# A routed-expert tail in fewer steps: logits made by tokens, fixed expert tiles indexed and gathered ahead of the spare ones, one batch's gated low parts on VectorE, routing masks by comparison

## The chip, the cores and the metric

The kernel runs on one core of a Trainium2 chip. The time is device microseconds of one execution. The core has five engines, which run their own instruction streams and wait for each other through semaphores: TensorE (PE in the profile; PEld is its weight load), VectorE (DVE), ScalarE (ACT), GpSimd (POOL) and SyncE (SP), which issues most of the DMA transfers.

## What is computed

Two batches of 512 tokens, 512 features wide, pass three residual blocks. All data are fp32.

```python
x = x + cross_attention(layernorm(x), ctx_1024)      # 8192 context rows, per batch
x = x + ssm(layernorm(x), ...)                        # long convolution by FFT, gated, clipped
x = x + ffn(layernorm(x), gate_w, gate_b, expert_w, expert_b)

def ffn(x, gate_w, gate_b, expert_w, expert_b):       # 8 experts of 512 x 512
    logits = xt @ gate_w + gate_b
    gates = softmax(logits)
    sel = argmax(gates)                               # one expert for each token
    onehot = one_hot(sel, 8)
    y_all = einsum('td,edh->eth', xt, expert_w) + expert_b[:, None, :]
    out = einsum('te,eth->th', onehot, y_all)
```

## The kernel before

The program is one long stream for each engine, written out by hand; there is no scheduler. It falls into a preparation of weights, an attention over the context for each batch, and a tail. The change is in the tail, the last 150 us.

Every result in PSUM is a job. The list `JOBS` sets the order of the jobs on TensorE and with it the bank of each (the number of the job modulo 8); a job waits until the job that had its bank before has been read. Large products are made of operands that are split into a high and a low part (`hl_A` to `hl_F`, fp32r): ScalarE rounds the high part, and VectorE or GpSimd subtracts to get the low part. A product is then 12 matmuls of 512 columns.

The tail, from about 978 us of the span on, does this:

- `outputs(c, groups)` on VectorE multiplies the spectra of the second batch (helper line 376 of the profile), `outputs_lo` (line 1810) takes low parts, `gate_output` (line 1823) gates the time signal. The low parts of the gated signal, `gated_lo`, are made on GpSimd for the first batch (line 2167) and on VectorE for the second (line 1815).
- `project_out` on TensorE (line 644) makes `x_ssm`, and `add_output` on VectorE adds it to the residual, tile by tile of 128 tokens, eight tiles.
- For each tile `turn_ffn` (line 978) transposes the sum on TensorE and ScalarE copies it (line 1224) into `spectra`. Both wait behind `weights(3)` in ScalarE's stream, which rounds expert matrix 3 once its DMA has landed.
- `gate_logits` (line 987) multiplies with the gate's weights. `gate_raw`, 8 columns, is the stationary operand, the tokens are the moving one, 512 or 256 at a time, so that the logits come out with experts on partitions. ScalarE copies them (line 1228), and `turn_logits` (line 998) transposes them to tokens on partitions.
- `scale_outputs`, `split_expert_bias` (lines 1895 to 1898) and `gate` (from line 1873) on VectorE give the one-hot of the chosen expert. `rank_tokens` on TensorE (lines 1007 to 1010) counts with two 0/1 masks, `before` and `ones`, where in its expert's queue each token stands. GpSimd makes the masks in `routing_masks` (lines 2192 to 2197).
- `route` on VectorE turns ranks into a place. There are 15 tiles of 128 places: 8 fixed ones, one for each expert, and 7 spare ones for what is over. It writes a 128x1024 0/1 matrix `place` (line 1928), `place_tokens` on TensorE (line 1017) makes the list of rows from it, and `gather_rows` and `scatter_rows` are converted (lines 1932, 1934).
- GpSimd gathers the rows of a tile with an indirect DMA (line 2202), after everything has been stored to `mixed` (`norm_stored`, `x_stored`). For each tile TensorE transposes the tokens (`turn_tokens`, line 1026), ScalarE rounds them (line 1347), VectorE takes the low part (line 1957), and `mix` multiplies with the expert's matrix (line 1040) and adds the bias (line 1045). GpSimd scatters the result (line 2209).

SyncE issues the loads and stores of this part in one fixed order: expert matrices 0, the bias, 1, 2 and 4, the store of x of batch 0, matrices 3 and 5, the store of x of batch 1, four stores of normalized rows, matrices 6 and 7, and then those of the spare tiles. GpSimd's order after the masks is: add the output bias to the residual of batch 1 (line 2162), low parts of matrices 0 to 3 (line 2023), gathers.

## Time and profile before

| | us |
|---|---|
| median of 3 executions | 1134.09 (1133.72 to 1135.25) |
| the profiled execution | 1134.54 |
| its span | 1132.8 |
| TensorE busy | 1093.9 (97%) |
| VectorE busy | 841.3 (74%) |
| ScalarE busy | 530.5 (47%) |
| GpSimd busy | 537.5 (47%) |

The span goes from the first to the last instruction of the trace, the execution's own time has 1.7 us around it. A busy share is a mean over a long program: in the stretch from 1040 to 1060 us TensorE is busy 12.4 of 20 us, and from 1060 to 1080 12.5 of 20. All times in this text are us from the span's start unless something else is said.

### The profile page before, as it was taken

What the parts mean: (1) busy time and instruction counts of PE and PEld (TensorE: products, weight loads), DVE (VectorE), ACT (ScalarE), POOL (GpSimd) and SP (SyncE); (2) the same over time, 40 slices, a digit from 0 to 9 for tenths busy, and PEclk for the clock granted to TensorE, in tenths of its full rate; (3) what the DMA queues carried; (4) which work ended last, traced back from release to release, by engine and by line L of the source; (5) the groups of instructions that cost most, each with busy time, mean ns of one, the idle gap of its engine ahead of it and who ended that gap; (6) DMA issues with size and microseconds to landing.
All of it is one profiled execution on the core that took longest, in us unless ns stands there. A gap on an engine that the chain in (4) does not pass through costs nothing.

```text
span 1132.8 us, 16497 instructions
## 1 busy us (share of the span) xinstructions
PE 1093.9 (97%) x4969; PEld 884.5 (78%) x4969; DVE 841.3 (74%) x1756; ACT 530.5 (47%) x1127; POOL 537.5 (47%) x588
## 2 busy tenths in 40 slices
PE   7999999999999999999999999999999999998498
PEld 5787877878888888888888888888888888886375
DVE  6963498799888888778357777776777657699584
ACT  4221056556555555533464444444444444356462
POOL 3700445345444544411266666665765632177253
PEclk8999999999999999999999999999999999999699
DMA  8211368977876787432429767766876541025991
GB/s 292 84 53 59 52 153 211 218 194 190 204 179 185 190 192 195 140 87 99 76 73 203 193 187 202 187 191 171 213 185 177 179 161 38 1 76 161 323 398 66
DMA packets 199351, 182.26 MB, mean 161 GB/s; under 512 B 17873, under 2 KB 144881, under 8 KB 199299
## 3 DMA queue, kind: packets, MB, share of 16 engines
q1 hardware_dynamic: 178658, 140.21, 48.3%
q10 hardware_dynamic: 17280, 31.46, 7.9%
q0 software_dynamic: 3360, 9.97, 2.4%
q8 instruction: 24, 0.39, 0.1%
q14 instruction: 29, 0.23, 0.1%
HBM read 141.73 MB, written 41.68 MB: 162 GB/s over the span
## 4 chain that ended last, share of the span: by engine, by line
PE 80%; DVE 8%; POOL 4%; DMA 3%; issue 3%; SPq 1%; ACT 1%; POOLq 0%; ACTq 0%; DVEq 0%
PE bank L644 39%; PE bank L783 28%; PE bank L1040 4%; PE bank L837 3%; PE bank L652 1%; PE bank L1026 1%; DMA stage<-in_L_xattn_hW_dram 1%; DVE h L1527 1%; DMA stage<-in_L_ffn_expert_w_dram 1%; DMA spectra<-in_ctx_dram 1%; PE bank L987 1%; PE bank L678 1%; POOL hl_C L2023 1%; PE bank L1045 1%; POOL hl_B L2039 1%
## 5 line engine op out<-in xcount | busy, mean ns | idle before, releaser
L1187 ACT ACTIVATE probs<-bank,nbias 128x512 f32<-128x512 f32 x128 | 88.1, 688 | 242.3 <-DVE nbias L1650 242.1
L783 PE MATMUL bank<-hl_F,probsT 128*128 128x512 f32 x768 | 190.4, 397 | 0.6 <-issue 0.4
L783 PE MATMUL bank<-hl_A,probsT 128*128 128x512 f32 x768 | 190.4, 396 | 0.0
L644 PE MATMUL bank<-hl_B,hl_D 128*128 128x512 f32 x768 | 185.7, 391 | 1.8 <-POOL hl_B L2039 1.4
L1645 DVE TENSOR_REDUCE mx<-bank 128x1 f32<-128x512 f32 x128 | 88.0, 687 | 133.9 <-PE bank L644 133.9
L644 PE MATMUL bank<-hl_C,hl_D 128*128 128x512 f32 x768 | 185.3, 390 | 0.0
L783 PEld LDWEIGHTS bank<-hl_F,probsT 128*128 128x128 f32 x768 | 144.1, 188 | 35.4 <-issue 0.8
L783 PEld LDWEIGHTS bank<-hl_A,probsT 128*128 128x128 f32 x768 | 144.1, 188 | 34.3 <-POOL hl_A L2032 0.2
L644 PEld LDWEIGHTS bank<-hl_B,hl_D 128*128 128x128 f32 x768 | 143.7, 188 | 34.1 <-issue 2.3
L644 PEld LDWEIGHTS bank<-hl_C,hl_D 128*128 128x128 f32 x768 | 144.1, 188 | 31.7 <-issue 0.3
L2032 POOL TENSOR_TENSOR hl_F<-stage,hl_F 128x512 fp32r<-128x512 f32 x64 | 84.7, 1323 | 162.2 <-ACT hl_F L1152 162.1
L2032 POOL TENSOR_TENSOR hl_A<-stage,hl_A 128x512 fp32r<-128x512 f32 x64 | 84.2, 1315 | 145.4 <-ACT hl_A L1152 145.4
L1691 DVE SCALAR_TENSOR_TENSOR rows<-rows,alpha,bank 128x512 f32<-128x512 f32 x128 | 90.9, 710 | 14.9 <-PE bank L783 14.9
L1662 DVE TENSOR_TENSOR probsT<-bank,probsT 128x512 fp32r<-128x512 f32 x128 | 87.3, 682 | 1.9 <-ACT probsT L1174 1.8
L1174 ACT ACTIVATE probsT<-bank 128x512 fp32r<-128x512 f32 x128 | 74.2, 580 | 10.8 <-PE bank L770 10.7
L1152 ACT ACTIVATE hl_F<-stage 128x512 fp32r<-128x512 f32 x64 | 40.4, 632 | 27.7 <-issue 18.2
L1152 ACT ACTIVATE hl_A<-stage 128x512 fp32r<-128x512 f32 x64 | 40.4, 632 | 27.6 <-issue 18.3
L2039 POOL TENSOR_TENSOR hl_C<-spectra,hl_C 128x512 fp32r<-128x512 f32 x32 | 40.9, 1292 | 22.9 <-ACT hl_C L1160 22.9
L2039 POOL TENSOR_TENSOR hl_C<-xb,hl_C 128x512 fp32r<-128x512 f32 x32 | 41.0, 1292 | 20.2 <-ACT hl_C L1160 20.2
L1667 DVE STREAM_TRANSPOSE bank<-resid 128x512 f32<-128x512 f32 x60 | 43.0, 716 | 9.4 <-DMA resid<-p_rows 9.4
L1683 DVE SCALAR_TENSOR_TENSOR lsum<-lsum,alpha,rsum 128x1 f32<-128x1 f32 x128 | 49.0, 383 | 0.0
L1699 DVE SCALAR_TENSOR_TENSOR zT<-h,cbdt,zT 128x512 f32<-128x512 f32 x64 | 46.6, 728 | 0.0
(419 smaller groups left out, 1862.6 us busy)
## 6 DMA issues: line engine op xcount, KB each, us to landing
p_rows<-probs ACTq DMA_DIRECT2D x120, 256.0 KB, 3.1
stage<-in_ctx_dram SPq DMA_DIRECT2D x112, 256.0 KB, 3.2
spectra<-in_ctx_dram SPq DMA_DIRECT2D x64, 256.0 KB, 5.9
xb<-in_ctx_dram SPq DMA_DIRECT2D x64, 256.0 KB, 5.9
resid<-p_rows SPq DMA_DIRECT2D x240, 64.0 KB, 2.1
h<-p_rows SPq DMA_DIRECT2D x120, 64.0 KB, 2.5
obB<-p_rows SPq DMA_DIRECT2D x120, 64.0 KB, 2.0
stage<-in_L_ffn_expert_w_dram SPq DMA_DIRECT2D x6, 1024.0 KB, 6.9
```

The source lines that it names most:

```text
L644: last = nc.tensor.matmul(dst, lhs[:, a, t, k * P:(k + 1) * P], rhs[:, c, t, :], start=(t == 0 and (a, c) == PASSES[0]), stop=(t == T - 1 ...
L783: last = nc.tensor.matmul(obank[u % 2][:], probsT[u % 2][:, a, j, :], nat[b][par][:, c, j, :], start=(j == 0 and (a, c) == PASSES[0]), sto ...
L1152: nc.scalar.activation(nat[b][par][:, 0, j, :], stage[par][:, j, :], ACT.Copy).then_inc(nat_hi, 1)
L1174: nc.scalar.activation(dst, src, ACT.Copy).then_inc(pT_hi, 1)
L1187: nc.scalar.activation(dst, src, ACT.Exp, bias=nbias[:, q:q + 1], scale=SCALE, accum_out=rsum[:, q:q + 1]).then_inc(probs_ready, 1)
L1645: nc.vector.tensor_reduce(mx[:, col], sbank[u % 2][:], AX_X, ALU.max).then_inc(stat_done, 1)
L1662: nc.vector.tensor_tensor(lo, src, hi, ALU.subtract).then_inc(pT_split, 1)
L1683: nc.vector.scalar_tensor_tensor(lsum[:, col], lsum[:, col], alpha[:, u:u + 1], rsum[:, col], ALU.mult, ALU.add).then_inc(sums_updated, 1)
L1691: nc.vector.scalar_tensor_tensor(rows[:, q, :], rows[:, q, :], alpha[:, u:u + 1], obank[u % 2][:], ALU.mult, ALU.add).then_inc(rows_added, 1)
L1699: nc.vector.scalar_tensor_tensor(kern[:, k, :], h[u % 2][:], weight, kern[:, k, :], ALU.mult, ALU.add).then_inc(term_added, 1)
L2032: nc.gpsimd.tensor_tensor(nat[b][par][:, 1, j, :], stage[par][:, j, :], nat[b][par][:, 0, j, :].bitcast(F32), ALU.subtract).then_inc(nat_s ...
L2039: nc.gpsimd.tensor_tensor(by_squares(ctxT[par][:, 1])[:, dd], square(squares[b][par], dd), by_squares(ctxT[par][:, 0])[:, dd].bitcast(F32) ...
```

## The change

The change has seven parts.

1. `gate_logits` swaps its operands: for each tile of 128 tokens the tokens are now the stationary operand (128 columns, four times, one for each 128 features), and `gate_raw` with its 8 columns is the moving one. The logits come out with tokens on partitions. The copies and `turn_logits` are gone. The logits of a tile follow two tiles behind its transposes.
2. `route` writes `place` twice: first by rank alone, for the fixed tiles, which `slots.0` turns into the rows of tiles 0 to 7, and then by lane, for the spare tiles (`slots.1`). GpSimd may gather tiles 0 to 7 after the first.
3. `split_expert_bias` moves from ahead of `gate` to behind `route`.
4. `turn_tokens(1)` moves from ahead of `mix(0)` into it, behind its first 3 matmuls.
5. The low parts of the first batch's gated signal move from GpSimd to VectorE, between groups 2 and 3 of the products.
6. `routing_masks` makes each mask with one comparison or multiply-add from `lanes`, without the wait for VectorE's products.
7. GpSimd takes the low part of expert matrix 0 ahead of the bias of batch 1, after a wait for VectorE's products.

The diff, cut to its core:

```diff
-             + tiles_at(0, "x_ssm")[2:] + tiles_at(1, "x_ssm") + tiles_at(0, "ffnT") + tiles_at(1, "ffnT")[:2]
-             + ["logits@0"] + tiles_at(1, "ffnT")[2:] + ["logits@1", "logit_columns", "ranks", "slots"] + MIX_JOBS)
+             + tiles_at(0, "x_ssm")[2:] + tiles_at(1, "x_ssm") + tiles_at(0, "ffnT") + tiles_at(1, "ffnT")
+             + ["logit_columns", "ranks"] + (["slots.0", "slots.1"]) + MIX_JOBS)
...
-                for t in range(T):
-                    turn_ffn(0, t)
-                for t in range(2):
-                    turn_ffn(1, t)
-                gate_logits(0, 1)
-                for t in range(2, T):
-                    turn_ffn(1, t)
-                gate_logits(1, 2)
-                turn_logits()
+                for n in range(B * T + 2):
+                    if n < B * T:
+                        turn_ffn(n // T, n % T)
+                    if n >= 2:
+                        gate_logits(n - 2)
                 rank_tokens()
-                place_tokens()
+                place_tokens("slots.0", 1, 0, E)
+                place_tokens("slots.1", 2, E, E)
                 turn_tokens(0)
                 for g in range(GROUPS):
-                    if g + 1 < GROUPS:
+                    if 0 < g < GROUPS - 1:
                         turn_tokens(g + 1)
...
+            def gate_logits(n):
+
+                dst = bank_of("logit_columns")
+                if n == 0:
+                    open_bank("logit_columns")
+                evacuated_from(f"ffnT.{n % T}@{n // T}")
+                for k in range(T):
+                    last = nc.tensor.matmul(dst[:, n * E:(n + 1) * E], spectra[:, n, k * P:(k + 1) * P], gate_raw[:, k, :],
+                                            start=(k == 0), stop=(k == T - 1))
+                if n == B * T - 1:
+                    last.then_inc(filled, 1)
...
+
+                pe.wait_ge(ranked, count)
+                dst = open_bank(job)
                 for n in range(B * T):
-                    last = nc.tensor.matmul(dst[:, 0:2 * E], place[:, n, :], numbered[:, n, :], start=(n == 0), stop=(n == B * T - 1))
+                    last = nc.tensor.matmul(dst[:, 0:width], place[:, n, :], numbered[:, n, first:first + width],
+                                            start=(n == 0), stop=(n == B * T - 1))
...
@@ -1039,6 +1028,8 @@
                     for a, c in PASSES:
                         nc.tensor.matmul(dst[:], tokens_hl[g % 2][:, a, t, :], weights[:, c, t, :],
                                          start=(t == 0 and (a, c) == PASSES[0]), stop=False)
+                    if g == 0 and t == 0:
+                        turn_tokens(1)
...
                 turned_ffn(0, range(T))
-                turned_ffn(1, range(2))
-                copy_logits(0)
-                turned_ffn(1, range(2, T))
-                copy_logits(1)
+                turned_ffn(1, range(T))
...
+            def gated_lo(b, k):
+                dve.wait_ge(gated_hi_done[b], k + 1)
+                nc.vector.tensor_tensor(gated_hl[b][:, 1, k, :], z[b][:, k, :], gated_hl[b][:, 0, k, :].bitcast(F32),
+                                        ALU.subtract).then_inc(gated_lo_done[b], 1)
...
+                nc.vector.tensor_tensor(numbered[:, :, 0:E], hits.bitcast(F32), of_token(token), ALU.mult)
                 link(nc.vector.tensor_tensor(hit_value, hits.bitcast(F32), of_expert(numbers[:, 0:E]), ALU.mult))
                 link(nc.vector.tensor_reduce(own, hit_value, AX_X, ALU.add))
...
-                nc.vector.tensor_reduce(rank, hit_value, AX_X, ALU.add)
+                link(nc.vector.tensor_reduce(rank, hit_value, AX_X, ALU.add))
+                place_at(rank)
                 link(nc.vector.tensor_tensor(above, count.unsqueeze(2).to_broadcast([P, E, SPARE]),
                                              limits.unsqueeze(1).to_broadcast([P, E, SPARE]), ALU.is_gt))
                 link(nc.vector.tensor_reduce(tiles_over, above, AX_X, ALU.add))
-                nc.vector.tensor_tensor(above, rank.unsqueeze(2).to_broadcast([P, B * T, SPARE]),
-                                        limits.unsqueeze(1).to_broadcast([P, B * T, SPARE]), ALU.is_ge)
                 link(nc.vector.tensor_tensor_scan(tiles_upto, unit, tiles_over, 0.0, ALU.mult, ALU.add))
+                filled_by(dve, "slots.0")
+                nc.vector.tensor_scalar(gather_rows[:, 0:E], bank_of("slots.0")[:, 0:E], float(FAR), float(TOKENS - 1),
+                                        ALU.add, ALU.min).then_inc(indexed, 1)
+                nc.vector.tensor_scalar(scatter_rows[:, 0:E], bank_of("slots.0")[:, 0:E], float(FAR), None, ALU.add).then_inc(evacuated, 1)
+                link(nc.vector.tensor_tensor(above, rank.unsqueeze(2).to_broadcast([P, B * T, SPARE]),
+                                             limits.unsqueeze(1).to_broadcast([P, B * T, SPARE]), ALU.is_ge))
                 nc.vector.tensor_reduce(over, above, AX_X, ALU.add)
                 link(nc.vector.scalar_tensor_tensor(extra, tiles_upto, float(E - 1), tiles_over, ALU.add, ALU.subtract))
-                nc.vector.scalar_tensor_tensor(lane, over, -float(P), rank, ALU.mult, ALU.add)
-                link(nc.vector.tensor_tensor(hit_value, hits.bitcast(F32), extra.unsqueeze(1).to_broadcast([P, B * T, E]), ALU.mult))
-                nc.vector.tensor_tensor(count, over, own, ALU.subtract)
+                link(nc.vector.scalar_tensor_tensor(lane, over, -float(P), rank, ALU.mult, ALU.add))
+                nc.vector.tensor_tensor(hit_value, hits.bitcast(F32), extra.unsqueeze(1).to_broadcast([P, B * T, E]), ALU.mult)
+                link(nc.vector.tensor_tensor(count, over, own, ALU.subtract))
                 link(nc.vector.tensor_reduce(rank, hit_value, AX_X, ALU.add))
                 link(nc.vector.tensor_tensor(count, count, rank, ALU.add))
                 link(nc.vector.scalar_tensor_tensor(count, over, 0.0, count, ALU.is_gt, ALU.mult))
                 link(nc.vector.tensor_tensor(group, count, own, ALU.add))
-                link(nc.vector.tensor_tensor(hit_group, group.unsqueeze(2).to_broadcast([P, B * T, 2 * E]),
-                                             numbers.unsqueeze(1).to_broadcast([P, B * T, 2 * E]), ALU.is_equal))
-                nc.vector.tensor_tensor(numbered, hit_group, token.unsqueeze(2).to_broadcast([P, B * T, 2 * E]), ALU.mult)
-                nc.vector.tensor_tensor(place, lane.unsqueeze(2).to_broadcast([P, B * T, P]),
+                link(nc.vector.tensor_tensor(hit_group, group.unsqueeze(2).to_broadcast([P, B * T, E]),
+                                             numbers[:, E:2 * E].unsqueeze(1).to_broadcast([P, B * T, E]), ALU.is_equal))
+                nc.vector.tensor_tensor(numbered[:, :, E:2 * E], hit_group, token.unsqueeze(2).to_broadcast([P, B * T, E]), ALU.mult)
+                place_at(lane)
+                choose_experts()
+                filled_by(dve, "slots.1")
+                nc.vector.tensor_scalar(gather_rows[:, E:GROUPS], bank_of("slots.1")[:, 0:SPARE], float(FAR), float(TOKENS - 1),
+                                        ALU.add, ALU.min).then_inc(indexed, 1)
+                nc.vector.tensor_scalar(scatter_rows[:, E:GROUPS], bank_of("slots.1")[:, 0:SPARE], float(FAR), None, ALU.add).then_inc(evacuated, 1)
+
+            def place_at(m):
+
+                nc.vector.tensor_tensor(place, m.unsqueeze(2).to_broadcast([P, B * T, P]),
                                         lanes.unsqueeze(1).to_broadcast([P, B * T, P]), ALU.is_equal).then_inc(ranked, 1)
...
@@ -1977,7 +1971,10 @@
                 outputs(1, range(1))
                 outputs_lo(0)
                 gate_output(0, range(2, T))
-                outputs(1, range(1, 5))
+                outputs(1, range(1, 3))
+                for k in range(T):
+                    gated_lo(0, k)
+                outputs(1, range(3, 5))
                 outputs_lo(1)
...
                 output_means(1)
                 dve.wait_ge(means_ready, 1)
                 scale_outputs()
-                split_expert_bias()
                 gate()
                 route()
+                split_expert_bias()
                 for g in range(2):
                     turned_lo(g)
                     weight_los(g + EARLY)
...
@@ -2187,14 +2178,9 @@
             def routing_masks():

                 filled_by(pool, "U1i.1@1")
-                pool.wait_ge(product_step, PRODUCTS * (TRIPS + 2))
-                whole = obB[:, 2 * P:3 * P]
-                chain(nc.gpsimd.memset(whole, 1.0))
-                nc.gpsimd.tensor_copy(ones, whole).then_inc(table_made, 1)
-                pool.wait_ge(table_made, 1)
-                chain(nc.gpsimd.affine_select(out=whole, in_=whole, compare_op=ALU.is_gt, fill=0.0, base=0,
-                                              pattern=[[1, P]], channel_multiplier=-1))
-                nc.gpsimd.tensor_copy(before, whole).then_inc(table_made, 1)
+                pool.wait_ge(iota_made, 1)
+                nc.gpsimd.tensor_scalar(ones, lanes, 0.0, 1.0, ALU.mult, ALU.add).then_inc(table_made, 1)
+                nc.gpsimd.tensor_scalar(before, lanes, partition, None, ALU.is_gt).then_inc(table_made, 1)
...
                 outputs_lo()
                 routing_numbers()
                 add_out_bias(0)
-                gated_lo()
                 routing_masks()
+                pool.wait_ge(product_step, PRODUCTS * (TRIPS + 2))
+                lo_tiles("W0", raw[BUF["W0"]], weights_hl[0])
                 add_out_bias(1)
-                for g in range(EARLY):
+                for g in range(1, EARLY):
                     lo_tiles(f"W{g}", raw[BUF[f"W{g}"]], weights_hl[g])
                 pool.wait_ge(x_stored, 16 * B)
                 pool.wait_ge(norm_stored, 16 * B * 2)
@@ -2225,6 +2212,7 @@
                 pool.wait_ge(indexed, 1)
                 for g in range(ROWS_KEPT):
                     gather(g)
+                pool.wait_ge(indexed, 2)
```

TensorE, the tail behind `project_out` (`L978` and `L974` are `turn_ffn`, `L987` and `L984` are `gate_logits`, `xb` holds the sums, `spectra` their transposes). Before:

```order
L978 MATMUL bank<-ident,xb 128x128 [waits evacuated]
L978 MATMUL bank<-ident,xb 128x128 x3
L987 MATMUL bank<-spectra,gate_raw 8x512 [waits copied,evacuated]
L987 MATMUL bank<-spectra,gate_raw 8x512 x3
L978 MATMUL bank<-ident,xb 128x128 [waits evacuated]
L978 MATMUL bank<-ident,xb 128x128 x3
L978 MATMUL bank<-ident,xb 128x128 [waits evacuated,copied]
L978 MATMUL bank<-ident,xb 128x128 x3
L987 MATMUL bank<-spectra,gate_raw 8x256 [waits copied]
L987 MATMUL bank<-spectra,gate_raw 8x256 x3
L987 MATMUL bank<-spectra,gate_raw 8x256 [waits copied]
L987 MATMUL bank<-spectra,gate_raw 8x256 x3
```

And with the change, from the third tile on:

```order
L974 MATMUL bank<-ident,xb 128x128 [waits evacuated]
L974 MATMUL bank<-ident,xb 128x128 x3
L984 MATMUL bank<-gate_raw,spectra 128x8 [waits copied]
L984 MATMUL bank<-gate_raw,spectra 128x8 x3
L974 MATMUL bank<-ident,xb 128x128 [waits evacuated]
L974 MATMUL bank<-ident,xb 128x128 x3
```

Six tiles were transposed ahead of the first logits; now three are, and each further tile stands behind the logits of an earlier one. The multiplication of 8 by 512 columns has become 128 by 8. The two groups of transposes of logits (`L998`) no longer follow.

VectorE, the end of `route` (`dft` is `place` and `numbered`, `ssm_in` and `ssm_w` hold small tables, `probsT` is the low part of the first tile's tokens). Before:

```order
L1925 TENSOR_TENSOR h<-ssm_in,ssm_w 128x128 [waits link_done]
L1927 TENSOR_TENSOR dft<-h,ssm_w 128x128 [waits link_done]
L1928 TENSOR_TENSOR dft<-ssm_in,ssm_w 128x1024
L1939 TENSOR_TENSOR ssm_in<-ssm_in,ssm_w 128x56
L1941 TENSOR_REDUCE ssm_w<-ssm_in 128x7 [waits link_done]
L1942 TENSOR_SCALAR ssm_w<-ssm_w 128x7 [waits link_done]
L1943 CAST chosen_expert<-ssm_w 128x7 [waits link_done]
L1944 TENSOR_SCALAR selected<-ssm_w 16x15
L1932 TENSOR_SCALAR gather_rows<-bank 128x15 [waits filled]
L1934 TENSOR_SCALAR scatter_rows<-bank 128x15
L1957 TENSOR_TENSOR probsT<-bank,probsT 128x512 [waits rounded]
```

With the change, the first placing (`L1927`) and its rows (`L1901`):

```order
L1891 TENSOR_TENSOR ssm_in<-onehot,bank 128x64 [waits filled,link_done]
L1892 TENSOR_REDUCE ssm_in<-bank 128x8
L1894 TENSOR_REDUCE ssm_in<-ssm_in 128x8 [waits evacuated]
L1927 TENSOR_TENSOR dft<-ssm_in,ssm_w 128x1024 [waits link_done]
L1896 TENSOR_TENSOR ssm_in<-ssm_in,ssm_w 128x56
L1898 TENSOR_REDUCE ssm_in<-ssm_in 128x8 [waits link_done]
L1899 SCALAR_TENSOR_TENSOR ssm_in<-ssm_w,ssm_in 128x8 [waits link_done]
L1901 TENSOR_SCALAR gather_rows<-bank 128x8 [waits filled,link_done]
L1903 TENSOR_SCALAR scatter_rows<-bank 128x8
```

And the second placing, with what stands ahead of the first tile's low part:

```order
L1938 TENSOR_SCALAR selected<-ssm_w 16x15
L1921 TENSOR_SCALAR gather_rows<-bank 128x7 [waits filled]
L1923 TENSOR_SCALAR scatter_rows<-bank 128x7
L1880 CAST dft<-probs 16x512 [waits iota_made,in_eb]
L1881 TENSOR_TENSOR h<-probs,dft 16x512 [waits link_done]
L1882 SCALAR_TENSOR_TENSOR probs<-h,ssm_w 16x512 [waits link_done]
L1883 SCALAR_TENSOR_TENSOR dft<-dft,ssm_w,probs 16x512 [waits link_done]
L1951 TENSOR_TENSOR probsT<-bank,probsT 128x512 [waits rounded]
```

The matrix `place` is written right behind the ranks and again 18 instructions later; the four instructions of the bias (`L1880` to `L1883`) now stand between the rows of the spare tiles and the first tile's low part.

## Rows read from the trace of the kernel before

**Rows 1.** The chain in order of time, from 985: start, us, what.

```profile
1028.13 7.80 DMA stage<-in_L_ffn_expert_w_dram
...
1038.15 1.95 ACT spectra L1224 x4
...
1040.23 3.59 PE bank L987 x8
...
1049.59 0.24 DVE logit L1876
...
1053.71 0.22 DVE ssm_in L1906
...
1057.27 1.15 DVE dft L1928
...
1058.46 1.89 PE bank L1017 x8
...
1060.37 0.18 DVE gather_rows L1932
...
1063.02 5.79 DMA spectra<-mixed,gather_rows
```

**Rows 2.** Timeline of VectorE: start, us, line, operation, count [idle before, releaser].

```profile
1001.54 1.67 DVE L376 TENSOR_TENSOR spectra<-probs,obB 128x512 f32<-128x512 f32 x1
...
1006.52 0.68 DVE L376 TENSOR_TENSOR obB<-resid,spectra 128x512 f32<-128x512 f32 x1
1007.12 0.68 DVE L376 TENSOR_TENSOR probs<-resid,spectra 128x512 f32<-128x512 f32 x1
...
1020.68 2.88 DVE L1815 TENSOR_TENSOR hl_A<-stage,hl_A 128x512 fp32r<-128x512 f32 x2
...
1043.76 0.41 DVE L1895 CAST dft<-probs 16x512 fp32r<-16x512 f32 x1
...
1046.36 0.20 DVE L1873 TENSOR_TENSOR ssm_in<-mv_out,gate_sums 128x64 f32<-128x64 f32 x1
```

**Rows 3.** Timeline of GpSimd.

```profile
994.20 11.85 POOL L2167 TENSOR_TENSOR hl_F<-zT,hl_F 128x512 fp32r<-128x512 f32 x4 [27.39 <-ACT hl_F L1288]
...
1010.00 2.16 POOL L2193 CAST dft<-obB 128x128 fp32r<-128x128 f32 x1
...
1017.85 6.85 POOL L2023 TENSOR_TENSOR hl_C<-stage,hl_C 128x512 fp32r<-128x512 f32 x4
```

**Rows 4.** Timeline of TensorE.

```profile
938.83 1.06 PE L897 MATMUL bank<-gate_raw,one 128*128 128x8 f32 x8
...
1034.63 2.78 PE L978 MATMUL bank<-ident,xb 128*128 128x128 f32 x24
...
1066.20 1.09 PE L1026 MATMUL bank<-ident,spectra 128*128 128x128 f32 x4 [5.86 <-DMA spectra<-mixed,gather_rows]
1068.95 1.09 PE L1026 MATMUL bank<-ident,spectra 128*128 128x128 f32 x4 [1.67 <-DMA spectra<-mixed,gather_rows]
...
1074.32 0.66 PE L1026 MATMUL bank<-ident,spectra 128*128 128x128 f32 x4
...
1078.14 0.66 PE L1026 MATMUL bank<-ident,spectra 128*128 128x128 f32 x4
```

**Rows 5.** Windows, TensorE alone: stretch, length, busy, granted clock, DMA share, GB/s.

```profile
931.90:938.80 6.90, 6.84 (x49) 1.00 0.32 123
...
1048.40:1051.90 3.50, 0.97 (x10) 1.00 0.51 195
...
1060.40:1066.10 5.70, 0.00 (x0) 0.50 0.94 326
```

**Rows 6.** Timeline of SyncE's DMA issues.

```profile
1053.27 1.77 SPq L560 DMA_DIRECT2D mixed<-zT  x2
```

**Rows 7.** Timeline of ScalarE.

```profile
1048.93 2.91 ACT L1330 ACTIVATE rows<-xb,ffn_shift,rstd 128x512 f32<-128x512 f32 x4
```

48 lines of the change are left out of this document (5 added, 43 removed).

## The prediction

> **What bounds the kernel now.** I read the page's busy lines first: TensorE is busy 97% of the whole span, so only a stretch where it waits can be shortened without taking work from it. The slices of the span show one, from 1036 to 1072. I followed the chain that ended last there in order of time, and then each engine's timeline. The reader is to see a relay [rows 1]: VectorE's work lets the load of expert matrix 3 start at 1028.13, it takes 7.80 us, ScalarE rounds that matrix and only then copies the transposed tiles (from 1038.15), TensorE multiplies them with the gate (from 1040.23), VectorE reads the logits at 1049.59, ranks at 1053.71, `place` at 1057.27, TensorE 1.89 us for the slots, rows at 1060.37, and a gather that took 5.79 us. From the second tile on TensorE repeats one pattern, 3.82 us a tile (1074.32 to 1078.14 [rows 4]), and waits for nothing: what arrives earlier at the first tile is worth its full amount at the end. The chain names GpSimd ahead of the load at 1028; the code says that the load stands behind the store of x of batch 0, which waits for VectorE's `add_output`. VectorE's own timeline has no idle time to speak of until it waits for the logits, so each microsecond there counts.
>
> **The change part by part.**
>
> *VectorE up to 1028.* Two SBUF operands on VectorE beside a GpSimd operation cost both engines: the four low parts of batch 0 took GpSimd 11.85 us [rows 3], and three of VectorE's products beside them took 1.67 us from the first at 1001.54 to the next ones, 4.98 for three until 1006.52, where such a product otherwise takes 0.60 to the next (1006.52 to 1007.12) [rows 2]. Without them VectorE gains 4.98 - 1.8 = 3.2. The four low parts then cost it 4 x 0.60 = 2.4; their high parts are rounded by then, no wait. The masks, two GpSimd operations of 128x128, move to when the last spectrum of batch 1 is made, about 986, beside VectorE's products. No row shows them there. Scaled by length (0.3 against 1.3 us) from the loss above, about 1.05 for each operation, they take 0.25 each, at least nothing: the cast at 1010.00 waited 2.16 us itself [rows 3] and VectorE lost nothing. I take 0.3. The low parts of matrix 0, now at about 1009 instead of 1017.85 [rows 3], meet `outputs_lo` (two SBUF operands, 2.4 us long). At worst two collide (2.1); if they behave as the cast, none does. I take 0.3, nearer the cast, whose neighbours were the same instructions. Later the bias of batch 1 stands where matrix 0 stood, beside `gated_lo` of batch 1, whose last two took 2.88 [rows 2]: same cost as before. Sum: -3.2 + 2.4 + 0.3 + 0.3 = **-0.2**, with bounds -0.8 and +1.9. The Trainium skill (SBUF — State Buffer, SBUF: two separate sides) says that the pair of ports is a lock held for the whole instruction, and that whoever starts first blocks the other. By it the moved low parts of matrix 0 could hold VectorE up by a whole operation each, 2.6 for two, in place of my 0.3.
>
> *Logits.* VectorE would be ready for them at 1043.8, when `scale_outputs` ends and the bias is no longer there (the CAST at 1043.76 [rows 2]). TensorE isn't. Copies still start at 1038.15; the first ends after 1.95/4 = 0.49, and TensorE starts 0.13 after a copy (1038.15 + 1.95 against 1040.23), at 1038.8 [rows 1]. Three tiles are transposed by then. What is left on TensorE is in series: eight gate products and five transposed tiles, since each transpose stands behind the gate product of an earlier tile. A tile of transposes is 2.78/6 = 0.46. The gate product in its new form has a twin in the trace: `gate_sums`, 128 columns stationary, 8 moving, fp32, four matmuls that are 8 records, 1.06 us with the last one's drain, and 8 x 0.116 = 0.93 without it, at the pitch of the transposes [rows 4]. So 8 x 0.93 + 5 x 0.46 + 0.15 = 9.9, the logits at 1048.7 in place of 1049.59: **-0.9**. What the swap saves in columns it pays in weight loads. Bounds: if it were 4 operations of 0.116 for a tile, 3.7 less, -4.6; that is near the end that VectorE sets (1044.0, -5.6). Upwards, the low clock: four transposes took 1.09 us at 1066.20, where 0.50 was granted [rows 4, 5], and 0.66 at 1074.32, 1.65 times with the drain in both; the levels themselves differ by 2. I take 1.8: 0.8 x 9.75 = +7.8, less 0.9, +6.9.
> The Trainium skill (TensorE: Matmul & The Clock Gate, LDWEIGHTS) has a load cost by the columns of the stationary operand, 128/1.2 ns. It speaks against the swap, from 8 columns to 128: by it eight loads a tile are 0.85 us, and the logits would come 0.6 earlier than by my row. The trace agrees within that.
>
> *Ranks to rows.* From the read of the ranks at 1053.71 to the start of `place` are 3.5 us today. The new first `place` needs only two reductions and a multiplication ahead of it, 0.6, since the extra multiplication for `numbered` lies under TensorE's ranks. So 0.6 + 1.2 (`place`) + 1.9 (slots, as before, it is loads again) and the rows at about 1057.5 in place of 1060.37: gathers can start 2.85 earlier, before what the earlier parts give. The gathers also wait for the stores of normalized rows. The last are issued by 1055.04 [rows 6]; 3 us for their 512 KB, an estimate from the 7.80 of a load of twice that beside others [rows 1], puts them down at 1058. ScalarE starts on those rows at 1048.93 [rows 7]. With the change its last copied tile comes at 1045.8 (1038.8, five gate products, five tiles, by the working above), the rows from 1046.4, 2.5 earlier: the stores end about 1055.5 and leave the gathers a margin of a microsecond.
>
> *But the first tile waits for more.* On TensorE `slots.1` stands ahead of the first transposes, and on VectorE the bias ahead of the first low part. With ranks at 1053.71: rows of tiles 0 to 7 until 1057.8, the rest of `route` as today, 3.6, to the end of the second `place` at 1061.4, slots 1.9, rows 0.3: 1063.6. Then the bias, 1046.36 - 1043.76 = 2.60 [rows 2], which was free ahead of the logits (VectorE waited 3.0 us there, 1046.56 to 1049.59) and isn't now: 1066.2. The first tile's own gather (1066.20 - 2.85 = 1063.35 [rows 4]), transposes 1.1 and copy 0.7 are ready at 1065.15, so the bias delays by 1.0. Low part 0.7: the first product can start at 1066.9. Today it is the second tile's transposes at 1068.95 [rows 4] that wait last, and with the transposes moved behind three matmuls the same work follows from 1066.9, if the second gather has landed: today 5.79 us after its issue at 1063.02 [rows 1], so 1066.0. It has. **-2.05.** From 1068.95 to 1074.32 [rows 4] the work is unchanged. I keep the low clock of that piece (0.50 while TensorE waits [rows 5]).
>
> The spare tiles' rows, matrix loads and scatters come in the same order and have a tile's time or more to spare. The loads of matrices 6 and 7, issued right behind those stores, move 2.5 to 3 earlier, the gathers 3.95, so they overlap about one microsecond more; the second gather has that to lose.
>
> Sum: -0.2 - 0.9 - 2.05 = **-3.15 us**. The profiled execution took 1134.54 (span 1132.8), 0.45 above the median 1134.09. 1131.4 against the former, **1130.9** as a median.
>
> **The rivals.**
>
> *The clock falls in the gate stage* (the other side). TensorE stood at 1.00 through 6.9 us of transposes alone and fell behind 3.5 us with 0.97 busy [rows 5]. The new stage is 9.9 us long; it is busy, but three quarters of it are weight loads with 8 columns behind them, and the engine idles 1.4 us longer ahead of it. No row has that for longer than the microsecond of `gate_sums`. If the clock halves after the first quarter, the remaining 7.4 us become 13.3: +5.9 - 3.15 = +2.75, 1136.8. It ends slower than before once more than 3.9 us of the stage's full-clock work run at the low clock (3.9 x 0.8 = 3.15). The Trainium skill (TensorE: Matmul & The Clock Gate, PE-mode transpose) says transposes don't count as busy; then nothing in the stage would hold the clock. The trace disagrees for transposes: the row of 6.9 us [rows 5]. It shows nothing for products of 8 columns.
>
> *Contention eats the rest.* VectorE collides with matrix 0 (+2.1 in place of 0.3) and the second gather lands a microsecond and a half late behind matrices 6 and 7: -3.15 + 1.8 to 2.5, 1132.7 to 1133.4, no measurable change. For it: DMA at 0.94 of its capacity while TensorE waited for the gathers [rows 5]. Against it: the same bytes stand ahead of the second gather, and they all move earlier.
>
> *The swap is cheaper than its twin* and VectorE's 1043.8 becomes the bound, or the first low part isn't held by the bias: -3.15 - 2.5, 1128.4. For it: a semaphore wait between groups gives loads time to run ahead. Against it: identical shapes in [rows 4].
>
> **How the numbers follow.** This kernel's executions can be told apart by about 0.2%, 2.3 us, so the bounds are 1131.8 and 1136.4. As forecast 0.45 (own range 1129.6 to 1132.1, of it nine tenths faster), cheaper 0.12 (faster), contention 0.20 (same), clock 0.23 (its price runs from a fraction of a microsecond to 7.8: half same, half slower). Nine tenths of 0.45 and 0.12 are 0.53 faster; 0.04, 0.20 and 0.11 are 0.35 same; 0.12 slower. The range leaves out a tenth at each end: 1128.6 to 1136.0.
>
> **What would show it.** Right: VectorE's `x_ssm` of batch 0 done within 0.5 us of 1027.6; TensorE without gaps between 1038.8 and 1048.6 at clock 1.00, 0.93 for each gate group; first gather 3.95 earlier; bias between second rows and first low part, VectorE never idle there; first product at about 1065.8, pitch 3.82 after. Wrong: a granted clock of 0.50 before 1048; products of VectorE over 1 us near 986 or 1009; a wait of TensorE for the second gather; GpSimd waiting for `norm_stored` rather than for the rows.

## The result and the profile after

| | before | after |
|---|---|---|
| median of 20 executions, us | 1135.66 | 1138.35 |
| profiled execution | 1134.54 | 1138.82 |
| its span | 1132.8 | 1136.7 |
| mean granted clock of the span | 0.985 | 0.980 |

The ratio is 1.0021, interval 1.0012 to 1.0029: the change makes the kernel slower by 2.4 us (the medians are 2.7 apart), where 3.15 us less were forecast. The executions of the changed kernel lie between 1133.93 and 1140.91, those of the kernel before between 1133.15 and 1138.63.

The chain of the changed kernel, in order of time (start, us, what), against [rows 1]:

```profile
1026.97 8.39 DMA stage<-in_L_ffn_expert_w_dram
...
1038.20 1.08 PE bank L984 x8
1039.28 0.95 PE bank L974 x4
1040.22 1.51 PE bank L984 x8
...
1050.04 4.93 PE bank L984 x24
1055.06 0.24 DVE logit L1860
...
1060.03 1.24 DVE dft L1927
1061.31 1.88 PE bank L1005 x8
1063.29 0.17 DVE gather_rows L1901
...
1069.21 0.33 DVE dft L1880
...
1072.55 1.62 PE bank L1029 x3
```

L984 is the gate product of one tile (8 records), L974 a tile of transposes. The first gate product takes 1.08 with its drain, the next 1.51; a pair with its transposes takes 2.45, where 0.93 + 0.46 were forecast. The logits are read at 1055.06, against 1049.59 before [rows 1]. From the ranks (1059.38) to the rows of the fixed tiles (1063.29) the path is as short as forecast. The windows of TensorE (stretch, length, busy, granted clock, DMA share, GB/s) show why the stage is slow:

```profile
1034.90:1038.20 3.30, 0.05 (x2) 1.00 0.00 0
1038.20:1039.50 1.30, 1.30 (x10) 0.82 0.00 0
1039.50:1055.00 15.50, 15.46 (x76) 0.50 0.54 184
1055.00:1076.40 21.40, 10.81 (x40) 0.50 0.88 294
```

TensorE waited 3.25 us, took up the gate products at 1.00, and the clock fell to 0.50 at 1039.1, 0.9 us later. From there it is busy without a gap, and the clock comes back only under the first tile's products, at about 1076.6. In the profile before the change it stood at 1.00 through the gate stage and fell at 1051.9, behind it [rows 5].

VectorE's and GpSimd's timelines, against [rows 2, 3]:

```profile
1000.86 2.48 DVE L1799 TENSOR_TENSOR hl_F<-zT,hl_F 128x512 fp32r<-128x512 f32 x4
1003.27 0.67 DVE L375 TENSOR_TENSOR spectra<-probs,obB 128x512 f32<-128x512 f32 x1
...
1008.09 1.28 DVE L1794 TENSOR_TENSOR hl_D<-spectra,hl_D 128x512 fp32r<-128x512 f32 x2
```

```profile
984.96 0.30 POOL L2182 TENSOR_SCALAR dft<-ssm_w 128x128 fp32r<-128x128 f32 x1 [18.88 <-PE bank L836]
985.25 1.57 POOL L2183 TENSOR_SCALAR dft<-ssm_w 128x128 fp32r<-128x128 f32 x1
```

The four low parts cost 2.48, and the products behind them take 0.67 again (1.67 to 1.78 before). Nothing of VectorE is held up from 1008 on, where GpSimd's low parts of matrix 0 now run.

TensorE's timeline at the first tiles, against [rows 4]:

```profile
1072.55 1.62 PE L1029 MATMUL bank<-hl_C,probsT 128*128 128x512 f32 x3 [2.37 <-DVE probsT L1951]
...
1078.24 0.66 PE L1015 MATMUL bank<-ident,spectra 128*128 128x128 f32 x4
```

The third tile's transposes stand at 1078.24 against 1074.32 [rows 4]: 3.9 us, the difference of the spans. All of the loss is made by then. One thing in that difference is not the change's: VectorE's first product of the second batch, ahead of every edit in the tail, started at 977.43 against 978.17. Over the 20 profiles of this text that start lies between 976.41 and 978.44, so a difference of two profiles has up to 2 us in it that no edit made. From that start to the third tile's transposes the changed kernel took 100.81, the kernel before 96.15: 4.7 more.

### The profile page after: what moved, and what is told of

Same layout as the page of the kernel before. It is cut to its first block, busy times and chain, and to the rows that moved or that the text cites. A ratio compares the mean times of both kernels' runs of the same rounds, so it can differ in the third digit from the quotient of the medians.

```text
span 1136.7 us, 16578 instructions
## 1 busy us (share of the span) xinstructions
PE 1101.8 (97%) x5009; PEld 897.9 (79%) x5009; DVE 841.6 (74%) x1764; ACT 529.6 (47%) x1125; POOL 529.3 (47%) x582
## 4 chain that ended last, share of the span: by engine, by line
PE 79%; DVE 10%; issue 3%; POOL 3%; DMA 2%; ACT 1%; SPq 1%; POOLq 0%; ACTq 0%; DVEq 0%
PE bank L643 38%; PE bank L782 28%; PE bank L1029 4%; PE bank L836 2%; PE bank L651 1%; PE bank L984 1%; DVE probs L375 1%; PE bank L1015 1%; DMA stage<-in_L_ffn_expert_w_dram 1%; DVE h L1511 1%; DMA spectra<-in_ctx_dram 1%; PE bank L677 1%; PE bank L1036 1%; POOL zT L2159 1%; DMA resid<-p_rows 1%
```

## The experiments

Theory: the gate stage ran at the low clock, and that alone is the loss. Rivals: the loss stands in the placing, the bias or the gathers; or it is on neither, and the low clock has another cause than the new products. Times are medians, ratios those to the kernel before on the same chip; the median of the kernel before lies between 1134.86 and 1135.75 in these comparisons, so two runs of different comparisons are better set side by side by their ratios. "Logits read at" is VectorE's first instruction on them. Every kernel is the changed one with the edit shown, unless said otherwise; only the runs with extra products do work that the reference has no use for, and none leaves any out.

### One part alone

**e1: former logits, the rest of the change kept** (`gate_logits(b, parts)`, `copy_logits`, `turn_logits` and their jobs put back).

> The changed kernel with the former logits (gate stationary, two copies, transposes) and all else of the change kept. Theory (the gate stage at the low clock is the whole loss): the copies start at 1037.5 and the logits are read at about 1048.9 in place of 1055.06, the rest of the path stays as in the changed kernel, so 6.2 us less: about 1132.2, ratio to the kernel before about 0.9975. Rival (the loss stands in the new placing, the bias or the gathers, and the logits only take time that is hidden): the time stays within 1 us of the changed kernel's, ratio 1.001 to 1.003.

1134.74, ratio 0.9998 (0.9985 to 1.0011). That is 2.6 us less than the changed kernel by the ratios and 3.6 by the medians, so the loss is the gate stage's, but not 6.2. Its windows show that the clock fell here too, in a wait of 3.8 us, and that it was back 3 us after the former products, 512 columns each, had begun:

```profile
1040.00:1041.00 1.00, 0.47 (x1) 0.54 0.00 0
...
1043.00:1044.00 1.00, 1.00 (x3) 0.76 0.19 61
1044.00:1045.00 1.00, 1.00 (x4) 1.00 0.90 260
```

The eight records of the first former product took 5.04 us where [rows 1] have 3.59. The logits came at 1051.34, 3.7 earlier than in the changed kernel, the first product only 1.9 earlier (1070.63): TensorE waited 3.06 us for the first gather. It was issued 1.35 us behind the rows; without a wait for the stores that is 1.10 (before the change, in the changed kernel and in e3), so the stores cost 0.25. The rest of the change, forecast at -2.25, was worth 0.2 us here.

**e2: the kernel before with the logits by tokens alone.**

> The kernel before with the logits by tokens alone. Theory (the stage at the low clock): the copies start at 1038.15, the logits are read 17.6 us later, at 1055.7 in place of 1049.59: +6.1 us, ratio about 1.0054, granted clock 0.50 from about 1040. If the clock falls only because of what else the change moves, the stage takes 9.9 us as forecast and the ratio is 0.999.

1140.34, ratio 1.0051 (1.0037 to 1.0066), six executions. The clock fell at 1039.6, two microseconds into the stage (window 1039 to 1040: 0.80), and stayed at 0.50. As the theory has it: the swap alone costs 5.8 us by the ratio, where I had forecast that it saves 0.9. The changed kernel is 3.4 us below this one, so with late logits the rest of the change was worth about that.

**x3: the kernel before with the moves on VectorE and GpSimd alone.**

> The kernel before with the moves on VectorE and GpSimd alone (low parts of batch 0 on VectorE, masks by comparison and earlier, low parts of matrix 0 ahead of the bias of batch 1). Forecast of the first text: -0.2 us (bounds -0.8 and +1.9), ratio 0.9998; by the profile of the changed kernel it is nearer -0.5, ratio 0.9996. Above 1.0010 the term was wrong.

1134.16, ratio 0.9996 (0.9981 to 1.0011), which can't be told from no change. In the profile the stretch from its first product (976.41, before 978.17) to `add_output` of batch 1 (1025.44, before 1027.61) is 0.41 shorter. This profile shows something else that bears on the theory. The gate stage in it is the former one, and it stands behind a wait of 2.74 us, as before (2.82). Here the clock fell all the same, 0.4 us into the stage, and was back at 1041.8 (TensorE's timeline and windows):

```profile
1038.00 5.29 PE L987 MATMUL bank<-spectra,gate_raw 128*8 128x512 f32 x8 [2.74 <-ACT spectra L1224]
```

```profile
1038.50:1041.80 3.30, 3.30 (x5) 0.50 0.30 42
1041.90:1044.00 2.10, 2.10 (x11) 1.00 0.94 272
```

So the former stage can lose the clock at this place too. It pays 1.7 us for it (5.29 against 3.59), since the clock comes back under its products; the new stage pays 7, since it doesn't.

### Other work ahead of the stage and in it

The same edit with other work in it, ahead of the first gate product, into a bank that the next transposes overwrite:

```diff
                 for n in range(B * T + 2):
...
+                    if n == 2:
+                        keep_busy("ffnT.3@0", 14)     # e3: 14 products, 512 columns, fp32r
+                        # x1: 3 x 4 products of 8 columns; x2: 6 tiles of transposes
                     if n >= 2:
                         gate_logits(n - 2)
+                        # e4: 2 of the 512-column products here (for n up to 8), v4: 1; e9: 2 here and none above
```

> The changed kernel with fourteen extra products (128x128 stationary, 512 columns, into a bank that the next transposes overwrite) in the 3.25 us in which TensorE waits for the first copy. They end before that copy does, so they cost nothing by themselves. Theory 'the idle time makes the clock fall': the stage then keeps 1.00, takes 9.9 us, logits at about 1048.2, 6.9 us less than the changed kernel: 1131.5, ratio 0.9968. Rival 'products of 8 columns don't hold the clock, whatever stands ahead of them': the fall comes a little later than 1039.5 but inside the stage; logits at 1052 to 1055, ratio 0.999 to 1.002.

> The changed kernel with the 3.25 us wait ahead of the gate stage filled by three more gate-like products of 8 columns (128x128 stationary, 24 records, 2.8 us). If 8-column products are as good as 512-column ones for the clock, it stays up as with the fourteen products (falls seen there at 1041.8 to 1046.6) and the time is near 1133.6. If they are no better than waiting, the clock falls at 1039 to 1040 as in the changed kernel: about 1138.

> The same wait filled by six more tiles of transposes (24 transposes, 2.8 us). If transposes hold the clock (as I read it from 6.9 us of them at 1.00 in the kernel before), the run is like that with the fourteen products, near 1133.6; if they don't, the clock falls at 1039 to 1040: about 1138.

| | ratio | interval | mean clock of its runs |
|---|---|---|---|
| e3, 512 columns | 0.9985 | 0.9974 to 0.9996 | 0.982 to 0.987 |
| x2, transposes | 1.0014 | 0.9998 to 1.0031 | 0.979 to 0.987 |
| x1, 8 columns | 1.0034 | 1.0019 to 1.0050 | 0.977 to 0.983 |
| changed kernel, waiting | 1.0021 | 1.0012 to 1.0029 | 0.978 to 0.984 |

Medians 1133.63, 1135.80, 1138.58, 1138.35; x1 and x2 ran on one chip, e3 on another. Windows of TensorE in e3, and then in x1:

```profile
1034.20:1037.50 3.30, 3.30 (x18) 1.00 0.00 0
1037.50:1046.00 8.50, 8.50 (x81) 1.00 0.53 167
1046.00:1047.00 1.00, 0.85 (x6) 0.65 1.05 410
```

```profile
1035.80:1038.60 2.80, 2.75 (x26) 1.00 0.02 9
1038.60:1040.10 1.50, 0.02 (x1) 1.00 0.00 0
1040.10:1041.00 0.90, 0.90 (x7) 0.81 0.00 0
1041.00:1042.00 1.00, 1.00 (x6) 0.50 0.00 0
```

In e3 the stage ran at 1.00 until its end (the fall is at 1046.3): from the first gate product at 1037.49 to the logits at 1046.96 are 9.5 us, my 9.9. So the working of the stage was right at the clock that it assumed. The gate products begin 0.7 us earlier than in the changed kernel, 0.5 of it by the start of the tail.

In x1 2.8 us of 8-column products helped nothing. Its profile is not a clean test of them, though: the copies came late in it, 1.53 us of waiting were left behind the extra products (none in e3, 0.47 in x2), and the clock fell at 1040.7, 0.6 us after that wait. How the other eleven executions stood is not shown. x2 lies between: its interval begins just above the end of e3's, and overlaps x1's. In its profile the clock fell at 1042.2, no earlier than in two profiles with the 512-column products (e7, e8). The page "TensorE: Matmul & The Clock Gate" of the Trainium skill (PE-mode transpose) says that a transpose "doesn't count as PE-busy the same way"; by that x2 would be like x1. The runs lean against it (2.8 us apart by the medians, overlapping intervals) without deciding it, and they lean against me too, who took the 6.9 us of [rows 5] to mean that transposes are as good as products.

e3's profile also shows what the change is worth with the clock held. Its third tile's transposes stand at 1071.24, 3.1 us earlier than before. That looks like the forecast, but 1.3 of it are the earlier start of its tail (976.90 against 978.17), and 1.8 are left. The ratio says 1.7.

**e9 and e4, v4: more dense work inside the stage.**

> The changed kernel with two extra products (512 columns) behind each of the eight gate products and none in the 3.25 us wait ahead of the stage. Theory 'the wait alone brings the clock down': it falls at about 1039.5 as in the changed kernel; if it then stays down to the end the stage takes 16.9 + 6.9 us, logits at 1061, ratio 1.0075. Theory 'it needs the wait and the light products together': the extra products hold it, or bring it back after a few microseconds as the former logits product did in its run (0.50 at 1041, 1.00 at 1044): logits between 1051.5 and 1055, ratio 0.999 to 1.002. In the kernel before the same 2 to 3 us of waiting stood ahead of dense products and no fall was seen.

1145.00, ratio 1.0073 (1.0050 to 1.0095), six executions; the first theory's figure was 1.0075. The clock was down at 1038.0, in the wait, 0.3 us ahead of the first gate product. Two dense products (the 512-column ones) behind each of the first seven gate groups (the text above says eight; the last had none) didn't bring it back in 24 us without a gap:

```profile
1037.00:1038.00 1.00, 0.00 (x0) 0.98 0.00 0
1038.30:1062.00 23.70, 23.70 (x98) 0.50 0.42 142
```

> The same fourteen, and two of the extra products behind each of the eight gate products. At the full clock each pair adds 0.43 us: the stage takes 9.9 + 3.4 = 13.3 us, logits at about 1051.5, 3.5 less than the changed kernel: 1134.8, ratio 0.9998. If the clock falls all the same, the stage takes 16.9 + 6.9 us, logits at 1061: ratio 1.0075. By the theory that light products lose the clock, this run keeps it where the fourteen alone don't; by the theory of the idle time both keep it and this one is 3.4 us slower than that.

> The kernel with the fourteen extra products and the bias ahead of the gate, and one extra product behind each gate product. It adds 1.7 us to the stage at the full clock. In four runs with the fourteen alone the clock fell inside the stage at 1041.9, 1041.8, 1044.1 and 1046.6. If one dense product a tile holds it, the logits come at about 1049.6 in every run, the time is about 1131.5 with a spread of 2 us instead of 4.5; if not, it is 2 us slower, 1133.5.

e4: 1133.93, ratio 0.9994 (0.9977 to 1.0010). v4, which has the bias ahead of the gate as well: 1132.81, 0.9985 (0.9966 to 1.0004). Both profiles stand at 1.00 through the whole stage (logits at 1049.95 and 1049.10), and both have one run in twelve at 1143.01 and 1142.44, with mean clocks of 0.980 and 0.981 where most others had 0.987 or more. With dense products in the stage the clock held in both profiles, and by the mean clocks in eleven executions of twelve. That the two slow ones paid for them at the low clock is read from their time and mean clock, no profile shows it.

### Without the wait

**e5 and v1: ScalarE copies the transposed tiles first**, matrix 3 is rounded behind the copies. v1 also moves the load of matrix 5 behind the stores and the bias behind the first low part.

```diff
-                weights(3)
                 turned_ffn(0, range(T))
-                turned_ffn(1, range(T))
+                for t in range(T):
+                    turned_ffn(1, range(t, t + 1))
+                    weights(3, range(t, t + 1))
```

> The changed kernel with ScalarE's copies of the transposed tiles ahead of the rounding of expert matrix 3, whose four operations stand one behind each copy of batch 1. So TensorE no longer waits for a load ahead of the stage. Theory (the idle time ahead of the stage makes the clock fall): the first copy starts at about 1034.1, the products follow the transposes without a gap, the clock stays 1.00, and the stage takes 9.9 us from 1034.9: logits at about 1044.9, 10.2 earlier than in the changed kernel and 2 earlier than with the fourteen extra products. About 1131.5 if nothing else takes it back. Rival 1 (light products lose the clock by themselves): logits at 1048 or later. Rival 2 (the rest of the path, from the logits to the first tile, waits for stores and gathers on full queues): the logits come as early as that and the first tile's transposes less than 1 us earlier than with the fourteen products.

> The kernel whose ScalarE copies the transposed tiles first, with two more edits: the load of matrix 5 stands behind the stores of x and of the normalized rows (in the earlier run it started at 1044.9, ahead of them, and the gathers had to wait for the stores until 1060.2), and the split of the expert bias stands behind the first tile's low part. Logits at about 1045.5, rows for the fixed tiles at 1053.8, stores down by 1055, first gather at about 1055 and landed at 1060 to 1061, first product at 1062.5 to 1063.5, 4 us earlier than the best so far: about 1128. Rival: the later load of matrix 5 or its bytes beside the gathers take it back: 1131 or more.

e5: 1134.63, ratio 0.9998 (0.9982 to 1.0015). v1: 1133.13, 0.9980 (0.9966 to 0.9994). In e5 the stage ran at 1.00 to its end and VectorE read the logits at 1045.90 without waiting; then the first gather was issued only at 1060.19, 6.1 us after its rows in place of 1.1. The load of matrix 5 (1044.93) now stood ahead of the stores, which took 8.0 us to land where v1's took 3.1, and TensorE waited 6.76 us for the gather: rival 2. In v1, the same stage with nothing ahead of it but products, the clock fell at 1037.9, with less than 4 us of the stage done:

```profile
1034.20:1037.00 2.80, 2.80 (x27) 1.00 0.00 0
1037.00:1038.00 1.00, 1.00 (x10) 0.95 0.90 340
1038.00:1048.20 10.20, 10.20 (x51) 0.50 0.32 118
```

So a wait isn't needed: the clock can fall in this stage with TensorE busy throughout. In e5 it fell at 1044.7, with the last records.

**v3: the same with the former logits.**

> The same, but with the former logits (gate stationary, 512 columns), which hold the clock. Logits products of batch 0 from 1036, of batch 1 from about 1039.5, logits read at 1043.5 to 1045, no low clock before it. If columns by the gate cost nothing here and the clock is what mattered, it is as fast as the new form with copies first or up to 2 us faster, 1126 to 1128, and its runs spread less. If the new form is worth something by itself, this one is slower by 1 us or more.

1131.20, ratio 0.9966 (0.9955 to 0.9978), the lowest ratio of all, with runs from 1130.53 to 1134.09. The clock stayed at 1.00 until 1047.2, behind the logits (read at 1045.92). Why not 1127: the gather took 7.6 us, and TensorE waited 3.23 us for it. The profile names the store as what released it (GpSimd's timeline), but it was issued 1.13 us behind the rows (1054.14), so the store cost it nothing:

```profile
1055.27 1.24 POOL L2210 DMA_INDIRECT spectra<-mixed,gather_rows  x1 [11.41 <-DMA mixed<-zT]
```

### The first tile

**e6: e3 with `split_expert_bias()` back ahead of `gate()`.**

> The changed kernel with the fourteen extra products ahead of the stage and the split of the expert bias back ahead of the gate, where VectorE waits 4.8 us. Forecast of the first text: the bias holds the first low part back by 1.0 us, so 1.0 less than with the fourteen products alone (1132.6 by the medians). Rival: the first tile's gather is the last to arrive, as in the profiled run with the fourteen products (transposes 1.64 us behind a DMA wait, low part 0.53 behind the copy): then nothing, 1133.6.

1131.59, ratio 0.9973 (0.9960 to 0.9986): 2.0 less than e3 by the medians, 1.4 by the ratios, whose intervals overlap. From the logits to the first product it is 16.65 us (1050.24 to 1066.89), against 17.49 in the changed kernel: there the bias cost 0.8. The 18.11 of e3 have a wait of 1.64 for the first gather in them. Its clock fell at 1044.1, not at 1046.3.

**e7: e6 with extra 512-column products in the five later waits; v6: v3 with them.**

> The same, and extra products also in the five later waits of TensorE (8 ahead of the ranks, 7 and 15 ahead of the two placings, 8 ahead of the first tile's transposes, 4 ahead of its first product), so that the clock should stay at 1.00 to the first tile. By the rows at either clock: ranks 2.0 to 1.0 us, two placings 1.87 to 0.93 each (the second only on the way to the first product), transposes 1.09 to 0.66, twelve products 3.7 to 2.9 with those that stand between them: the first gather is issued 2 us earlier and the first tile ends 3 to 4 us earlier: about 1129.5. Rival: the gathers on full queues set the first tile: 1 to 1.5 us less only. Rival: the extra products overshoot the waits and cost up to 1 us each.

> The fastest kernel so far (former logits, copies first, matrix 5 behind the stores, bias behind the first low part) with extra 512-column products in the five later waits of TensorE (8, 7, 15, 12 and 4). With the clock at 1.00 the ranks take 1.0 less and the first placing 0.9 less, the transposes 0.4 less and the first tile's products 0.9 less. The stores and the gathers don't move (the gather is issued when the stores are down, at 1055.3, and takes 6 to 7.6 us), so only the last two count: 1.3 us, about 1130; if the stores come down earlier than the rows, up to 3 us, 1128.5. Rival: overshoot of the extra products, 1131.2 or more.

e7: 1131.99, ratio 0.9967 (0.9949 to 0.9984), runs from 1127.34 to 1136.39. In its profile, which is the slowest of its twelve executions, the clock fell at 1041.6 inside the stage, and then the extra products ran at half speed and overshot (the eight ahead of the ranks took 3.76 us). v6: 1131.12, 0.9970 (0.9954 to 0.9986), mean clocks of 0.993 to 0.998, and no faster than v3: the rows are there at 1052.29, but the gather is issued at 1055.10, here 1.7 us late by the stores, and TensorE waits for it until 1064.05.

**e8, v7, v8: matrix loads held back.** e8 is e6 with matrices 6 and 7 held until the second gather is down; v7 and v8 are v6 with 5, 6 and 7 held until the first and the second, and with five extra products ahead of the first tile's transposes in place of twelve.

> The kernel with the fourteen products and the bias ahead, and the loads of matrices 6 and 7 (2 MB) held until the second gather has landed. Theory (the first gather takes 6.2 us because it shares the queues with these loads): it lands 2 to 4 us after its issue, the first product then waits for the second placing and comes about 1.5 us earlier than without, 1131 to 1132. Rival: a gather takes 5 us or more by itself; then no change, or a loss if matrix 6 comes late.

> The last kernel (former logits, copies first, extra products in the later waits) with the loads of matrices 5, 6 and 7 held until the first gather has landed. Theory (the queues hold the gather): the stores are down a microsecond earlier, the first gather is issued at about 1054 and lands in 4 to 5 us, at 1058.5; the second placing ends at 1057.1; first product at 1060.5 to 1062 in place of 1066.5, if the second gather is not caught behind the loads: about 1127. Rival: the loads come late by 6 us and a later tile waits for matrix 5 to 9, so that it is given back: 1130 to 1132, with waits of TensorE for ScalarE or VectorE behind a matrix after 1080.

> The same with the loads held until the second gather has landed, some 1.3 us later. If the second gather is caught behind the loads in the other run, this one is faster, else up to 1 us slower; the rival as there.

e8: 1135.29, ratio 0.9994 (0.9975 to 1.0014); in its profile TensorE waited 1.1 us in all for low parts of the spare tiles from 1105 on, where e6 waited for nothing. v7: 1134.22, 0.9984 (0.9969 to 0.9999). v8: 1135.53, 0.9994 (0.9979 to 1.0008). The gather of v7 was down 4.7 us after its issue (9.0 in v6) and the first product stood at 1061.61, 4.9 earlier than in v6. Then (TensorE's timeline, and ScalarE's):

```profile
1076.23 1.19 PE L1055 MATMUL bank<-hl_D,probsT 128*128 128x512 f32 x2 [6.33 <-DVE probsT L1985]
```

```profile
1071.73 2.19 ACT L1358 ACTIVATE hl_A<-stage 128x512 fp32r<-128x512 f32 x4 [8.12 <-DMA stage<-in_L_ffn_expert_w_dram]
1073.83 1.06 ACT L1364 ACTIVATE probsT<-bank 128x512 fp32r<-128x512 f32 x2
```

ScalarE stood at the rounding of matrix 5, which had come late, with the third tile's copy behind it: all of it was given back, and more. What was won at the first tile was lost by the late loads.

## Why the prediction was wrong

- **VectorE up to 1028** (-0.2): right, and a little better, -0.4 in both profiles (reckoned from a start that is 0.7 earlier in the changed kernel and 1.8 in x3). The masks cost 0.1 to 0.2; matrix 0 cost VectorE nothing, so neither my 0.3 nor the 2.6 of a whole held instruction came. But the reading that each microsecond there counts was too simple: the load began 1.16 earlier, took 8.39 in place of 7.80, and the copies began 0.58 earlier.
- **Logits** (-0.9): the step that failed. The count of 9.9 us in series was right at full clock (9.5 in e3). Run at 0.50 from 1039.1 it was 16.86, from the first product at 1038.20 to 1055.06: 6.96 more. Between forecast (-3.15) and profile (+3.9) lie 7.05; what else there is nearly cancels (gate products 0.4 earlier than forecast, 0.2 more from the logits to the first product, 0.3 more in the first tile's products). The bound that I drew for a low clock was 7.8 more for the stage (the 6.9 has the -0.9 in it), so it covered what came; the sum used none of it. From start to start a gate group took 0.82 in e3 and 1.56 in the changed kernel, the transposes 0.47 and 0.89: 1.9 times for both, where I took 1.8.
- **The rival of the clock** had the place and the mechanism, with a chance of 0.23 and a price "after the first quarter" of 5.9. The choice against it was wrong in three ways. I read [rows 5] as holding for the stage because transposes had held, but there was no 8-column product among them, and the stage's own records held the clock for less than 4 us in v1. The 1.4 us by which TensorE was to idle longer were a slip: it starts 1.4 us earlier and has 1.4 us less work ahead, so by my own figures the wait stays at 2.8; it was 3.25. And that wait is enough with no change to it: x3 lost the clock behind 2.74 us. What I never priced was the way back. The former products had the clock again after 3.4 us (x3 and e1); the new stage hadn't after 15.
- **Ranks to rows** (3.9 in place of 6.66): right, 3.91 (1059.38 to 1063.29).
- **The first tile**: from the logits to the first product 17.3 forecast (1049.59 to 1066.9), 17.49 measured; the bias holding it by 1.0, nearly right (0.8 by e6). The second gather had landed, right: TensorE shows no wait ahead of 1073.96. With earlier logits the first gather is the last to arrive: 18.11 in e3, 0.8 more than forecast. And the products behind it took 6.17 to the third tile's transposes, where I kept the 5.37 of before: their granted clock was 0.59 in the mean, against 0.68.
- **The stores' margin** of a microsecond: not tested by the changed kernel, since its logits came late. It held in e3, whose logits came 1.5 earlier than forecast (1.3 of it by the start of its tail): the gather was issued 1.10 behind the rows, as without any store to wait for. It was used up where the rows came at 1054.1 or earlier: by 0.03 us in v3, 1.2 in v7 and v8, 1.7 in v6 (and 0.25 in e1). So it isn't what kept the -2.05 from e3; the 0.8 and 0.8 of the term above are.
- **Bounds**: what stayed unsure is the spread. The changed kernel's executions lie 7 us apart; the fastest has a mean clock of 0.984, the slowest of 0.978. The point at which the clock falls changes from run to run. The Trainium skill ("TensorE: Matmul & The Clock Gate", The HAM clock gate) says "run-variable" of the clock's rise at a kernel's start. Here the fall varies too: in four profiles of the stage behind the same fourteen products it came at 1041.6, 1041.8, 1044.1 and 1046.3 (e7, e8, e6, e3). The kernel before spreads over 5.5 us itself, and x3 against [rows 5] shows the same stage with a fall and without one.

**Still open**: what makes the clock fall, and where. It fell in a wait (e1, e9), soon after one (the changed kernel, x1, x3), two microseconds after one (e2) and with no wait at all: after under 4 us of the stage in v1, after 9 in e5 and e3. Each is one profiled execution. How far transposes hold it. Whether 8-column products in a wait that they fill wholly are worth anything. The extra products alone, without any part of the change, were not run.

## What to carry to other kernels

A TensorE stage that is busy is not a stage at full clock. When work is turned round into other shapes, price the stage at both clocks, and ask two things of rows that have these very shapes: whether the clock holds through them, and whether it comes back under them once it is down. Here a fall cost the former shapes 1.5 to 1.7 us (e1, x3) and the new ones 7. And a gain at the head of a relay is only as long as the next queue allows: stores behind a load put off a gather by 5.0 us (e5), three loads ahead of a gather made it 4.3 longer (v6 against v7), and a load held back for the gather took back 4.9 (v7).

## What the runs showed of the hardware

- Fourteen products of 512 columns in the wait ahead of the stage: ratio 0.9985, where waiting gives 1.0021. 24 records of 8 columns with 128x128 loads (busy 2.75 of 2.80 us, with 1.5 us of waiting left behind them in the profile): 1.0034.
- At 0.50, with three tenths of the time in dense products (e9), the clock didn't return in 23.7 us, nor in 15.5 us of gate products and transposes (the changed kernel). Under fp32 products of 512 columns with 8 stationary ones it returned 3.0 us (e1) and 3.8 us (x3) after they began.
- At 0.50 against 1.00, gate products (1.56 against 0.82 us) and transposes (0.89 against 0.47) took 1.9 times as long.
- A gather by itself was down in 4.7 us, behind three matrix loads in 9.0 (v7, v6).
- GpSimd's four low parts of matrix 0 took 7.24 us beside VectorE's products and low parts, where those of matrix 2 took 5.07; VectorE's two-operand instructions there kept their pitch of 0.60 (the changed kernel, from 1008.24 on).
